# Six graph layers pipelined on one core: GpSimd finds the join's deviation between the halves of an item's result, and two units' exponentials stand later on ScalarE

## What is computed

```python
# layer 0: 8 heads of 32 features
q, k, v = x @ Wq + bq, x @ Wk + bk, x @ Wv + bv
scores  = where(adj == 0, -inf, q_h @ k_h.T / sqrt(32))       # for each head h
x       = norm(x + concat_h(softmax(scores) @ v_h) @ Wo + bo) * gamma + beta
# layer 1: one head of 256
scores  = where(adj == 0, -inf, (x Wq) (x Wk).T / sqrt(256))
x       = norm(x + softmax(scores) (x Wv) Wo + bo) * gamma + beta
# layers 2 to 5: one head of 128, values are x itself
scores  = where(adj == 0, -1e10, (x Wq.T + bq) (x Wk.T + bk).T / sqrt(128))
x       = norm(x + (softmax(scores) x) Wc.T) * gamma + beta
```

## Time and profile before

| | |
|---|---|
| median of 3 runs | 2533.27 us (2532.14 to 2534.21) |
| the profiled execution's own time | 2531.23 us |
| its span, first to last instruction | 2529.4 us |
| busy: TensorE, VectorE, ScalarE, GpSimd | 94%, 61%, 62%, 73% |
| mean granted TensorE clock | 0.990 of full speed |
| one turn of five slots, in the middle | 38.07 us |

### The profile page before, as it was taken

The page is one execution under the profiler, slowest core; times in us unless marked ns, Lnnn a source line. Parts: engine busy times, 40 slices in busy tenths (PEclk is TensorE's granted clock), DMA queues, the critical chain, the costliest instruction groups (busy, mean ns, idle before and its releaser), DMA issues.

```text
span 2529.4 us, 57112 instructions
## 1 busy us (share of the span) xinstructions
PE 2382.8 (94%) x20944; PEld 2182.5 (86%) x20944; DVE 1553.4 (61%) x4874; ACT 1570.5 (62%) x5512; POOL 1841.4 (73%) x2439
## 2 busy tenths in 40 slices
PE   5899999999999999999999999999999999999985
PEld 4789889889889889889889889889888888888874
DVE  2566666666666666666666666666666666666663
ACT  4666666666666666666666666666656656656642
POOL 3577777777777777777777777777777777777773
PEclk8999999999999999999999999999999999999997
DMA  3000000000000000000000000000000000000000
GB/s 141 22 26 22 24 31 22 25 30 20 27 31 18 28 31 18 28 31 18 29 30 18 28 30 18 28 30 18 28 31 18 29 31 18 28 31 12 14 10 13
DMA packets 38150, 68.62 MB, mean 27 GB/s; under 512 B 4336, under 2 KB 12656, under 8 KB 37232
## 3 DMA queue, kind: packets, MB, share of 16 engines
q1 hardware_dynamic: 37872, 64.97, 7.5%
HBM read 48.18 MB, written 16.78 MB: 26 GB/s over the span
## 4 chain that ended last, share of the span: by engine, by line
PE 58%; DVE 13%; ACT 12%; POOL 12%; issue 3%; DMA 0%; DVEq 0%; SPq 0%; POOLq 0%
PE qk_bank L374 12%; PE value_bank L382 11%; ACT probs L607 8%; PE unit_bank L374 7%; PE context_bank L527 6%; PE unit_bank L437 4%; POOL rstd L909 4%; PE qk_bank L480 4%; PE unit_bank L382 4%; DVE xT_lo L771 4%; POOL x_out L928 3%; POOL x_out L930 3%; PE unit_bank L449 3%; DVE y L825 2%; DVE y L806 2%
## 5 line engine op out<-in xcount | busy, mean ns | idle before, releaser
L928 POOL TENSOR_TENSOR x<-y,rows 128x512 f32<-128x512 f32 x320 | 407.9, 1275 | 280.2 <-DVE y L825 280.2
L825 DVE TENSOR_SCALAR y<-y,mv,rstd 128x256 f32<-128x256 f32 x768 | 280.7, 408 | 362.1 <-POOL rstd L909 362.0
L627 ACT CAST xT_hi<-qk_bank 128x512 fp32r<-128x512 f32 x320 | 191.2, 598 | 449.7 <-PE qk_bank L480 449.7
L374 PE MATMUL qk_bank<-xT_hi,w_lo 128*128 128x256 f32 x1280 | 405.4, 317 | 67.0 <-DVE xT_lo L771 67.0
L930 POOL TENSOR_TENSOR x<-x,rows 128x512 f32<-128x512 f32 x320 | 412.5, 1289 | 25.1
L607 ACT ACTIVATE probs<-unit_bank,negmax 128x128 f32<-128x128 f32 x1024 | 366.0, 384 | 49.9 <-DVE negmax L743 49.9
L382 PE MATMUL value_bank<-w_lo,xT_hi 128*128 128x256 f32 x1280 | 393.1, 307 | 0.0
L806 DVE SCALAR_TENSOR_TENSOR y<-context_bank,rtotal,x 128x256 f32<-128x256 f32 x640 | 277.2, 474 | 155.6 <-PE context_bank L527 155.6
L374 PE MATMUL qk_bank<-xT_lo,w_hi 128*128 128x256 f32 x1280 | 361.7, 283 | 0.0
L382 PE MATMUL value_bank<-w_hi,xT_lo 128*128 128x256 f32 x1280 | 361.6, 283 | 0.0
L374 PE MATMUL qk_bank<-xT_hi,w_hi 128*128 128x256 f32 x1280 | 360.5, 282 | 0.0
(11 more groups left out here) (89 smaller groups left out, 6339.1 us busy)
## 6 DMA issues: line engine op xcount, KB each, us to landing
x0T<-xT_in SPq DMA_DIRECT2D x64, 256.0 KB, 2.6
x<-x_in SPq DMA_DIRECT2D x64, 256.0 KB, 2.6
out<-x_out SPq DMA_DIRECT2D x64, 256.0 KB, 2.1
adj<-adj_in SPq DMA_DIRECT2D x64, 128.0 KB, 2.2
rows<-rows_in SPq DMA_DIRECT2D x1, 1920.0 KB, 11.4
probs0T<-w_in SPq DMA_DIRECT2D x1, 1024.0 KB, 5.1
probs<-w_in SPq DMA_DIRECT2D x1, 1024.0 KB, 8.1
x<-w_in SPq DMA_DIRECT2D x1, 1024.0 KB, 14.0
```

The lines of the kernel that those rows point to most:

```text
L374: mm = pe.matmul(psum[:, n * G * N:(n + 1) * G * N], split(w, name, kd, at, at + P), flat(xT_half[:, kd]), start=kd == 0 and w is w_lo, st ...
L825: m = dve.tensor_scalar(y[:, r, g], y[:, r, g], mv[:, r, g, 0:1], rstd[:, r, g:g + 1], ALU.subtract, ALU.mult)
L928: pool.tensor_tensor(new, y[:, r], row_of_each(f"gamma{layer}"), ALU.mult).then_inc(zg_ready, 1)
```

## The change

On ScalarE, `exp0` of unit 1 moves from the end of slot 4 to slot 0, behind `softmax`, where `exp0` of unit 2 stood; `exp0` of unit 2 moves to the end of slot 0, behind `move_probsT`; and `move_v` in slot 0, which stood between `softmax` and `exp0`, now comes after `exp0` of unit 1. On VectorE, unit 1's reciprocal moves behind `reciprocal_total`, ahead of unit 3's row maximum. On GpSimd, unit 1's products move behind `find_rstd` of the item, and `scale_and_shift` is cut in two, `scale` (L928) and `shift` (L930): in slot 3 the order becomes scale of the item, `find_rstd` of the join, shift of the item, scale and shift of the join. TensorE's and SP's lists are as they were.

```diff
--- before.py
+++ after.py
@@ -685,12 +685,10 @@
                     split_x0T(group)
                 if item(i - 1):
                     softmax(i - 1)
-                if item(i - 1) and late_values(i - 1):
-                    move_v(i - 1)
                 if (group := due(i, 6)) is not None:
                     exp0(group, 0)
                 if (group := due(i, 5)) is not None:
-                    exp0(group, 2)
+                    exp0(group, 1)
                 if (group := due(i, 4)) is not None:
                     move_probs0T(group, 1)
                     exp0(group, 3)
@@ -698,12 +696,14 @@
                     move_q0(group)
                 if (group := due(i, 7)) is not None:
                     move_k0(group)
+                if item(i - 1) and late_values(i - 1):
+                    move_v(i - 1)
                 if item(i):
                     move_qk(i)
                 if item(i - 1):
                     move_probsT(i - 1)
-                if (group := due(i, 6)) is not None:
-                    exp0(group, 1)
+                if (group := due(i, 5)) is not None:
+                    exp0(group, 2)
                 if (group := due(i, 3)) is not None:
                     move_probs0T(group, 3)
                 if i == -7:
@@ -849,7 +849,6 @@
                 if (group := due(i, 5)) is not None:
                     reciprocal0(group, 0)
                     row_max0(group, 2)
-                    reciprocal0(group, 1)
                 if (group := due(i, 4)) is not None:
                     reciprocal0(group, 2)
                 if item(i - 1) and item(i - 1)[0] == 1:
@@ -862,6 +861,7 @@
                 if (group := due(i, 6)) is not None:
                     row_max0(group, 1)
                 if (group := due(i, 5)) is not None:
+                    reciprocal0(group, 1)
                     row_max0(group, 3)
                 if (group := due(i, 9)) is not None:
                     move_v0(group)
@@ -915,19 +915,23 @@
                                            rtotal0[:, j, g].unsqueeze(2).to_broadcast([P, QUADS, N]), ALU.mult)
                 m.then_inc(probs0_ready, 1)
 
-            def scale_and_shift(norm):
+            def result(norm):
                 layer, group = layer_and_group(norm)
-                r = NORM_AT[norm] % YS
-                if layer == LAYERS - 1:
-                    new = x_out[:, group % STORES]
-                    if group >= STORES:
-                        pool.wait_ge(stored[group % STORES], 16 * (group // STORES))
-                else:
-                    new = x[:, group % HELD]
+                return x_out[:, group % STORES] if layer == LAYERS - 1 else x[:, group % HELD]
+
+            def scale(norm):
+                layer, group = layer_and_group(norm)
+                if layer == LAYERS - 1 and group >= STORES:
+                    pool.wait_ge(stored[group % STORES], 16 * (group // STORES))
                 pool.wait_ge(z_ready, NORM_AT[norm] + 1)
-                pool.tensor_tensor(new, y[:, r], row_of_each(f"gamma{layer}"), ALU.mult).then_inc(zg_ready, 1)
+                pool.tensor_tensor(result(norm), y[:, NORM_AT[norm] % YS], row_of_each(f"gamma{layer}"),
+                                   ALU.mult).then_inc(zg_ready, 1)
+
+            def shift(norm):
+                layer, group = layer_and_group(norm)
                 pool.wait_ge(zg_ready, NORM_AT[norm] + 1)
-                pool.tensor_tensor(new, new, row_of_each(f"beta{layer}"), ALU.add).then_inc(x_ready, 1)
+                pool.tensor_tensor(result(norm), result(norm), row_of_each(f"beta{layer}"),
+                                   ALU.add).then_inc(x_ready, 1)
 
             def split_later(n):
                 pool.wait_ge(later_hi_ready, n + 1)
@@ -940,7 +944,6 @@
             for i in SLOTS:
                 if (group := due(i, 5)) is not None:
                     normalise_probs0(group, 0)
-                    normalise_probs0(group, 1)
                 if (group := due(i, 4)) is not None:
                     normalise_probs0(group, 2)
                 if (group := due(i, 3)) is not None:
@@ -951,13 +954,20 @@
 
                 if item(i - 2):
                     find_rstd(("item", i - 2))
+                if (group := due(i, 5)) is not None:
+                    normalise_probs0(group, 1)
                 if item(i - 1):
                     keep_valid(i - 1)
                 if item(i - 2):
-                    scale_and_shift(("item", i - 2))
+                    scale(("item", i - 2))
+
                 if (group := due(i, 2)) is not None:
                     find_rstd(("group", group))
-                    scale_and_shift(("group", group))
+                if item(i - 2):
+                    shift(("item", i - 2))
+                if (group := due(i, 2)) is not None:
+                    scale(("group", group))
+                    shift(("group", group))
                 if i == FIRST:
                     pool.wait_ge(rest_loaded, 48)
                 if i in (-4, -3):
```

## The result

The changed kernel takes 2499.35 us (median of 4 runs, 2498.83 to 2501.86) against 2532.93 us for the kernel before in runs beside it: ratio 0.9869, 95% interval 0.9852 to 0.9886. That is 33.6 us less, faster as forecast, but 0.56 us a turn over 60 turns where 1.43 were forecast, and outside the range of 2422 to 2490 us.

What follows compares the result with a forecast made beforehand. TensorE, busy 94%, was taken as the bound. Unit 0's transposes 1.43 us sooner a turn, times 60, is 86 us; 2531.2 less 86 is 2445, the median 2 above: 2447 us. Range 2425 to 2472, for 8 in 10 2422 to 2490.

Steps and rivals of the forecast that it cites:

- the three losses: TensorE's lost time at A, B and C, waiting for `xT_lo` twice and `kT` once: together 2.03 of 38 us a turn.
- A: TensorE in slot 4, context's first matmul to projection's end: 3.01 us against 2.27 undisturbed; the 0.74 lost would go.
- B: TensorE's start of the transposes behind slot 4's projection: 0.50 us lost a turn, of which 0.1 to 0.2 would stay.
- C: TensorE in slot 0, context's first matmul to projection's end: 3.06 us against 2.27; the 0.79 lost would go.
- D: New wait in slot 0: TensorE's value bank waits for `move_v` behind unit 1's exponentials; 0.26 us plus 0.1 refill.
- Unit 1's products: GpSimd would finish them at 1219.35, before TensorE transposes unit 1's weights at 1219.9: slack 0.5 us.
- The early deviation: GpSimd in slot 3: the join's rstd, found ahead of layer 5's shift, would be ready 1.02 us sooner.
- I take no cost: VectorE's normalise (L825) running beside GpSimd's shift of the item was costed at nothing.
- the first rival: VectorE's normalise and GpSimd's shift exclude each other: gain only 0.21 us a turn, 2520 us; chance 0.07.
- The prediction's own sign for it: For the first rival: L825 longer, or later than rstd, by over 0.1.
- The second rival: Only ScalarE's part works, as the join's statistics come later and GpSimd waits: 0.44 us a turn, 2507 us; chance 0.09.
- 60 turns: Of 64 groups, 60 turns were taken to have the whole gain of 1.43 us, 86 us; count 58 to 62.

Runs made afterwards that it cites:

- the late shift: Changed kernel with layer 5's shift moved two slots later, to the end of slot 0, no longer beside the join's normalise: 2449.5 us (ratio 0.9667).

## Why the prediction was wrong

- **The bound and the three losses**: right in place, too large in size. A is 0.62 of the 0.74, B 0.25 of the 0.50, C 0.75 of the 0.79.
- **C** went, as forecast, with the exponentials of unit 1. **D** came, as forecast: 0.24 a turn where 0.36 was worked out. Unit 1's products came in time, as worked out; the wait that could have followed didn't.
- **The early deviation** came 1 us sooner, as forecast, at GpSimd. The step that failed is the next, "I take no cost" for the normalise beside the shift: a term put at nothing. It cost 0.94 us at the first L825 (1.35 against 0.41) and 0.84 a turn on TensorE's stretches (10.35 against 9.51 with the late shift), all but 0.05 of what A and B had to give. The argument was that an instruction of 408 ns, as long as the statistics', can't be one that excludes GpSimd. The duration showed the pace of the instruction and not what it excludes: with constants the same form takes 290 ns, with scalars from memory 408, and at 408 it is held all the same. That the aggregation ran beside GpSimd was true and proved nothing about another form.
- **The rival** that named this got 0.07, and its time, 2520, was too high by 21 us. It began both L825 anew 0.1 after the shift; in fact the first stands ready and ends 0.15 behind the shift, the second 0.32 later, so what waits for the normalise was 0.03 sooner than before and not 0.27 later: 0.56 a turn, not 0.21. The prediction's own sign for it, L825 longer than 0.41 by over 0.1, is the one that came. The second rival is nearest in time (2507) and has slot 4 as before, but not for its reason: the join's statistics were in time and the deviation 1 us early.
- **What stood in the trace before and was read past**: "The trace doesn't show VectorE's normalise (L825) beside a long GpSimd product" is true of L825 and not of its operation. While the pipeline fills, another plain `tensor_scalar`, the one that makes the mask of `adj` with two constants (L738), starts beside a long GpSimd product twice:

```profile
94.68 1.26 POOL L930 TENSOR_TENSOR x<-x,rows 128x512 f32<-128x512 f32 x1
129.71 1.18 POOL L914 TENSOR_TENSOR probs<-probs,rtotal 128x256 f32<-128x256 f32 x2
```

```profile
95.64 0.45 DVE L738 TENSOR_SCALAR mask<-adj 128x256 bf16<-128x256 int32 x1
130.40 0.64 DVE L738 TENSOR_SCALAR mask<-adj 128x256 bf16<-128x256 int32 x1
```

```profile
L738 DVE TENSOR_SCALAR mask<-adj x64: 260/273/644, 18.9 to 2374.1; 128x256 bf16<-128x256 int32 x64
```

Its median of 64 is 273 ns; these two took 448 and 644, and both ended 0.15 us behind the GpSimd instruction, as L825 did later. That is the first rival's mechanism, in the trace before the change, with its price. Nor did GpSimd always idle beside L825: in 250 of the 768 its `keep_valid` (L900, two columns, 0.2 us) ran beside it.

```profile
1213.33 0.20 POOL L900 TENSOR_TENSOR rtotal<-rtotal,valid 128x2 f32<-128x2 f32 x1
```

```profile
1213.40 0.74 DVE L825 TENSOR_SCALAR y<-y,mv,rstd 128x256 f32<-128x256 f32 x2 [0.49 <-POOL rstd L909]
```

Those L825 took 0.41 us like the others (all 768 lie between 381 and 416 ns). That is no proof of freedom: a hold that ends 0.15 behind so short a neighbour would be over, by an estimate from these rows, at 1213.68, before L825's own end at 1213.81. The range of the forecast didn't hold the first rival's time.

- **60 turns**: right to one turn. 0.55 a turn in the timeline against 33.6 us is 61; 1.39 in the run with the late shift against 84.3 us is also 61.

## What to carry to other kernels

Before two instructions of VectorE and GpSimd are moved beside each other, look for rows in which the same operations overlap already, the filling of the pipeline and other lines of the kernel included, and compare the longest of a group with its median; if there is none, the cost can be as much as the length of the neighbour. In these runs a plain `tensor_scalar` from SBUF to SBUF, and a `scalar_tensor_tensor` of two columns with two operands in SBUF, were held until GpSimd's long instruction ended; so place such forms where GpSimd idles or runs its short ones, let VectorE start first, or give the work to ScalarE. When an engine's busy time rises with unchanged instructions, read the maximum of its durations: a held instruction counts as busy.

## What the runs showed of the hardware that was not expected

- `tensor_scalar` on fp32 takes 0.41 us for 256 columns with two scalars from memory and 0.29 with constants. The first, no faster than the statistics over as many columns (0.41), lasts 1.35 us beside a GpSimd product; it ends 0.15 us behind it.
- A VectorE instruction of two columns with two SBUF operands took 1.22 us beside a GpSimd product of 512 columns, 0.16 without it.
- A GpSimd memset, which reads nothing, holds the plain `tensor_scalar` too: the two L825 took 1.75 us together.
- Started while an L825 ran, GpSimd's product lost 0.1 us, while an L825 started during that product lost 0.94: here the short instruction on VectorE was the cheap neighbour, the long one on GpSimd the dear one.
- ScalarE's two activations over the same tile took 1.09 us together, beside GpSimd's product and without it.
- Not every long GpSimd instruction holds: in the kernel before, the `tensor_scalar` of two columns that finds `valid` (L750, median 0.16 us) took 0.49 once beside a product of 4.56 us, but 0.16 both times that it lay beside the rstd instruction, which lasts 0.71 for two columns.
